# Delta stage: rows normalised and transposed ahead of the systems, and split behind the last substitution step

## What is computed

```python
h = _rms(x, attn_norm_w)
q = silu(silu(_causal_dwconv(h @ Wq.T, conv_q)))   # k and v alike
q = _l2norm(q.reshape(B, T, nh, hd))               # k alike; 32 heads of 16
beta = jax.nn.sigmoid(h @ Wbeta.T)
def step(S, inp):
    kt, qt, vt, bt = inp
    err = jnp.einsum('bhvk,bhk->bhv', S, kt) - vt
    S = S - bt[..., None, None] * err[..., None] * kt[..., None, :]
    o = jnp.einsum('bhvk,bhk->bhv', S, qt)
    return (S, o)
S, o = jax.lax.scan(step, S0, (km, qm, vm, bm))
x = x + _rms(o, out_norm_w) @ Wout.T
```

## Time and profile before

| what | value |
|---|---|
| median of 3 runs | 3093.07 us (3091.05 to 3095.14) |
| profiled execution | 3089.57 us |
| its span | 3087.7 us |
| VectorE busy | 1990.8 us, 64% |
| TensorE busy | 2757.9 us, 89% |
| ScalarE busy | 1436.7 us, 47% |
| GpSimd busy | 1009.8 us, 33% |
| delta phase in the span | from about 570 to 1690 us |

### The profile page before, as it was taken

The page is one execution under the profiler, slowest core; times in us unless marked ns, Lnnn a source line. Parts: engine busy times, 40 slices in busy tenths (PEclk is TensorE's granted clock), DMA queues, the critical chain, the costliest instruction groups (busy, mean ns, idle before and its releaser), DMA issues. The chain is left out here.

```text
span 3087.7 us, 66709 instructions
## 1 busy us (share of the span) xinstructions
PE 2757.9 (89%) x26968; PEld 1466.9 (48%) x26968; DVE 1990.8 (64%) x2991; ACT 1436.7 (47%) x2378; POOL 1009.8 (33%) x713
## 2 busy tenths in 40 slices
PE   6999999686888888888855999999999699999997
PEld 3444444252544444444433444444444366666664
DVE  3444444459989898898993544545543377777775
ACT  2222222375767758667632432222222256666664
POOL 0000000107538346274481000000000177777776
PEclk9999999888998989889866999999999899999998
DMA  6999888500000000000040032332120111111110
GB/s 241 336 334 332 312 284 310 176 15 1 2 29 2 29 13 19 29 2 29 16 155 21 22 111 94 101 104 96 66 71 28 66 38 41 41 41 41 41 37 31
DMA packets 126284, 290.20 MB, mean 94 GB/s; under 512 B 30480, under 2 KB 35216, under 8 KB 121968
## 3 DMA queue, kind: packets, MB, share of 16 engines
q1 hardware_dynamic: 122608, 261.85, 24.4%
q10 hardware_dynamic: 3456, 25.17, 2.4%
HBM read 244.96 MB, written 42.01 MB: 93 GB/s over the span
## 5 line engine op out<-in xcount | busy, mean ns | idle before, releaser
L2141 POOL TENSOR_TENSOR d_zb<-d_za 128x1024 f32<-128x1024 f32 x32 | 75.3, 2354 | 955.7 <-DVE d_za L2203 955.7
L899 PE MATMUL b_e<-b_hT,s_region 128*128 128x512 f16 x1152 | 283.3, 392 | 49.1 <-DVE s_region L1327 36.5
L1629 PE MATMUL c_r<-c_hT,c_g_pair 128*128 128x512 f16 x1056 | 244.4, 382 | 1.6 <-DVE c_hT L1805 1.6
L2008 PE MATMUL d_m<-s_region,d_xiT 128*128 128x512 bf16 x1024 | 238.4, 384 | 5.1 <-ACT d_xiT L2121 1.6
L1629 PE MATMUL c_r<-c_hT,c_u_pair 128*128 128x512 f16 x1056 | 242.3, 379 | 0.0
L1629 PE MATMUL c_d<-c_d_pair,c_aT 128*128 128x512 f16 x1056 | 242.1, 379 | 0.0
L1819 DVE SCALAR_TENSOR_TENSOR c_av<-c_r,c_sg 128x512 f32<-128x512 f32 x88 | 60.8, 691 | 271.7 <-PE c_r L1629 211.2
L1327 DVE SCALAR_TENSOR_TENSOR s_region<-b_e,b_cw,s_region 128x496 f32<-128x496 f32 (+2 forms) x288 | 203.0, 716 | 18.3 <-ACT s_region L1117 9.9
L851 POOL TENSOR_TENSOR b_tmp<-b_L,s_hn 128x496 f32<-128x496 f32 (+30 forms) x124 | 122.5, 988 | 260.9 <-ACT b_L L1100 251.5
L851 POOL TENSOR_TENSOR b_tmp<-b_L,b_U 128x496 f32<-128x496 f32 (+30 forms) x124 | 130.8, 1055 | 223.8 <-ACT b_L L1100 214.4
L899 PEld LDWEIGHTS b_e<-b_hT,s_region 128*128 128x128 f16 x1152 | 104.0, 100 | 190.0 <-DVE s_region L1327 44.2
(11 more groups left out here) (255 smaller groups left out, 6029.7 us busy)
## 6 DMA issues: line engine op xcount, KB each, us to landing
a_cT<-in_ctxT SPq DMA_DIRECT2D x128, 512.0 KB, 9.7
a_cn<-in_ctx SPq DMA_DIRECT2D x128, 512.0 KB, 9.1
a_x_ln<-in_x SPq DMA_DIRECT2D x8, 1024.0 KB, 16.1
a_cw<-in_ctx SPq DMA_DIRECT2D x128, 64.0 KB, 9.5
a_x_res<-in_x SPq DMA_DIRECT2D x32, 256.0 KB, 11.4
x<-a_x_out SPq DMA_DIRECT2D x32, 256.0 KB, 11.3
b_xg<-x SPq DMA_DIRECT2D x8, 1024.0 KB, 5.5
om<-b_hT SPq DMA_DIRECT2D x32, 256.0 KB, 2.0
```

The lines of the kernel that those rows point to most:

```text
L899: mm = pe.matmul(p[:], w_qkv[:, a, i, n, c * P:(c + 1) * P], hp[:, b, n, :], start=(n + a + b == 0), stop=(n == DC - 1 and a == 1))
L1629: mm = pe.matmul(out, x, y, start=start and i == 0, stop=stop and i == 2)
L2008: mm = pe.matmul(p[:], xiT[:, c, :], w[:, c, j * 512:(j + 1) * 512], start=(c == 0), stop=(c == DC - 1))
L2141: nc.gpsimd.tensor_tensor(o[:, :, 0, :], a[:, :, 0, :], a[:, :, 1, :], ALU.add).then_inc(bf, 1)
```

## The change

In the body k of the delta phase:

- PE transposes V0 to V3, then the rows of group k + 1, then waits for the last Gram bank, then L0 to L7. Before, L0 to L4 stood ahead of the rows and L5 to L7 behind.
- ACT copies right sides 0 and 1, normalises the rows of group k + 1, copies right side 2, takes the rows' high halves, copies right side 3 and then systems 0 to 7. Before, all right sides came first, then the normalising, systems 0 to 4, the high halves, eight masks, systems 5 to 7.
- Those eight masks now stand with the next sixteen, behind the first taps and the copies of U.
- VectorE splits the low halves of group k + 2 behind step 30 instead of step 24.

Nothing is added or removed; every instruction has the same shape as before. `LE` is no longer used. The MLP phase is the same in both kernels.

```diff
--- before.py
+++ after.py
@@ -994,13 +994,11 @@
                     pe.wait_ge(vt_ready, DC * (k + 1))
                     for i in range(NV):
                         turned(k, f"V{i}", lambda d: vt[:, :, d])
-                    E.used(pe, 0, f"{k}.gram{DC - 1}.{BG - 1}")
-                    for i in range(LE):
-                        turned(k, f"L{i}", lambda t: Gs[:, t, :])
                 if nxt:
                     rows(g)
                 if cur:
-                    for i in range(LE, NL):
+                    E.used(pe, 0, f"{k}.gram{DC - 1}.{BG - 1}")
+                    for i in range(NL):
                         turned(k, f"L{i}", lambda t: Gs[:, t, :])
                 if nxt:
                     E.used(pe, 0, f"{g}.h{DC - 1}")
@@ -1205,12 +1203,12 @@
                 prev, cur, nxt = k >= 1, 0 <= k < NG, k + 1 < NG
                 g = k + 1
                 if cur:
-                    for i in range(NV):
-                        right_side(k, i)
-                    if nxt:
-                        rows_normal(g)
-                    for i in range(LE):
-                        system(k, i)
+                    right_side(k, 0)
+                    right_side(k, 1)
+                if cur and nxt:
+                    rows_normal(g)
+                if cur:
+                    right_side(k, 2)
                 if nxt:
                     rows(g)
                 if k < 0:
@@ -1219,8 +1217,8 @@
                     high_weights("v")
                     act.wait_ge(w_ready, PAIRED["q"])
                 if cur:
-                    masks(k, 0, 8)
-                    for i in range(LE, NL):
+                    right_side(k, 3)
+                    for i in range(NL):
                         system(k, i)
                 if nxt:
                     tap_first(g, "q", 0)
@@ -1236,7 +1234,7 @@
                 if not cur and prev:
                     squares_first()
                 if cur:
-                    masks(k, 8, 24)
+                    masks(k, 0, 24)
                 if nxt:
                     betas(k)
                     tap_first(g, "q", 1)
@@ -1422,7 +1420,7 @@
                 for s in range(S - 1):
                     if cur:
                         solve(k, s)
-                    if s == 24 and g + 1 < NG:
+                    if s == S - 2 and g + 1 < NG:
                         low_rows(g + 1)
                     if nxt and s == 0:
                         convolve(g, "q", 0)
```

## The result

The changed kernel took 3064.31 us (median of 4 runs, 3061.35 to 3070.18), the kernel before beside it 3094.11 us: a ratio of 0.9907, 95% interval 0.9889 to 0.9924, 29.8 us faster (23.5 to 34.3 by the interval). Forecast were 3066.0 us and 27.1 us. The profiled execution took 3061.35 us, the shortest of the four, and has a span of 3059.6 us, 28.1 less than before.

A forecast was written before the change was run, and what follows sets the result against it. VectorE sets the pace, so only its idle time can be won. Six seams at 3.6 us, first 3.4, last 3.3, less 1.2, give 27.1 us: 3093.07 to 3066.0 us, range 3050 to 3080.

The forecast's parts named there:

- a loss of 1.2: Behind the seam: ScalarE's square and the projection of chunk 3 come late, taken as 0.2 us a cycle in six cycles.
- the late clock: Output projection late in the cycle: at low clock cycles are 3.5 us longer; no more or fewer long cycles expected.
- the allowances: At each seam: 0.5 us for a clock fall and 0.3 for the load's landing, making 4.4 us saved 3.6.
- the ring: Old seam: VectorE's split waits for ScalarE's high halves, and system 7's copy waits for step 29, which stands behind that split.
- ScalarE's chain: At the seam, ScalarE's copies in the new order are next late: 4.4 us saved, not 7.45; VectorE keeps about 3.4 idle.
- The wait for hc: Ahead of normalising the rows: hc lands at 1038.5, deciding by 0.1 us; another seam's load would put 1.4 on the path.
- even odds: TensorE's new 3.4 us pause while rows are normalised: clock falls or not, a fall costing 1.0 us, so 0.5 a seam.
- the slack of system 7's transpose: TensorE at the seam: system 7 turned near 1048.0 against 1048.6 needed, 0.6 us slack, reducing a clock fall's 1.6 us cost.
- Rival B: As the forecast, but the long cycles become short: four more times 3.5 us, 3052 us; chance 0.14.
- C: Win partly given back: clock falls or TensorE's round trip, 1.5 us a seam, or root 1.2 late each cycle; 3078, chance 0.20.
- D: Slower: half clock holds through chunk 0's projections, 10.7 instead of 5.35 us, chunk 3's projection 6.5 late; 3104, chance 0.05.
- E: VectorE starts as ever, system 7's copy held by something the rows do not show; 3087 to 3093, chance 0.05.

The follow-up runs named there:

- the kernel with the later masks: Changed kernel with twelve masks instead of 24 ahead of ScalarE's squares and nineteen instead of seven behind: 3055.0 us, ratio 0.9877; with the eight matmuls 3044.41 us.

## Why the prediction was right

**The sum.** Forecast were 27.1 us, measured 29.8. By VectorE's starts in the profiles the first seam gave 3.35 us (forecast 3.4), the six others with rows 19.8 (21.6 forecast), the last 3.2 (3.3): 26.4 against 28.3. The bodies gave 3.7 us where a loss of 1.2 was forecast, because one long cycle fewer was met. So the mechanism and its sizes held within 2 us, and that the profiled total lies above the forecast and not below it is luck of the late clock.

**The seam.** Its terms came out one by one: right sides 0 and 1 at 0.98 us instead of 0.88, the normalising 2.83 as forecast (2.8), the high halves 2.98 instead of 2.29 (two waits of 0.17 us for TensorE), the eight systems 4.05 instead of 3.90. Start of the next system: forecast 12.8 us behind the first right side at full clock and 13.6 with the allowances, measured 13.60. The 7.45 us wait went and 4.04 us came back at line 1098, where 3 to 4 were forecast. The order with the masks behind gives 26 of the 30 us, the split and the masks by themselves 0 and 5. The prediction named the ring and got ScalarE's chain right; it didn't say that most of its 4.4 us a seam are the 3.4 us of masks.

**The load.** The wait for hc decided as forecast: nothing at four of the six seams, 0.35 and 1.07 us at two, 0.24 on the mean where 0.3 was taken. The seam of 27.3 us is the one with 1.07.

**The clock in the pause.** It fell at all six seams, where even odds were taken, and cost 0.8 where 1.0 was taken. The 0.5 us of the sum was low by 0.3. The cost came by another way than the slack of system 7's transpose: ScalarE waited for the rows' transposes in the high halves.

The prediction read the length of the gap as what decides: 2.52 us in the old seam, followed by full speed "in six seams of seven". The rows don't bear that out. Of the seven it was five, since at the second the 16 transposes took 2.96 us at a granted clock of 0.72. And the other kernels with the old order had the same gap, 2.50 to 2.53 us, at each of the six seams, behind the same instructions: behind it the transposes ran at full speed throughout at all six with the masks alone, at two of six with the split alone, and at none of six with the eight matmuls in the kernel before. So the even odds were a guess and not a reading.

**First and last seam.** 3.3 us at the first and 3.4 in the last cycle (120.2 to 116.8), forecast 3.4 and 3.3; the masks alone bring them. The first one differs between executions of the old order too: 27.3 us in the kernel before, 25.9 and 25.8 with the split alone and with the matmuls.

**Behind the seam.** ScalarE's square was forecast 24.6 us behind the start; TensorE's sums began at 24.5:

```profile
1073.15 1.13 PE L916 MATMUL b_r<-s_xa,b_heads 128*32 128x512 f32 x4 [1.92 <-ACT s_xa L1126]
```

Here a step failed. I took a gap of about 2.6 us ahead of the projection of chunk 3 as one that keeps the clock and set the loss at 0.2 us a cycle. The gap came ahead of the sums instead. It was 1.9 us in five cycles, and behind it the granted clock went to the lower level in four of them (0.58 to 0.61 over the next 4 us). In exactly these four the root came late:

```profile
1100.10 3.35 DVE L1338 RECIPROCAL s_region<-s_region 64x512 f32<-64x512 f32 x1 [0.80 <-ACT s_region L1153]
```

The wait is 0.8 us each. In the two of cycles 2 to 7 in which the clock stayed up there, VectorE did not wait for the root at all. So the odds were wrong. But the wait is not what it costs. Two short cycles have it, the fourth and the fifth, and their bodies are 93.5 us, against 93.2 in the second, which has none, and 93.1 and 93.2 in the short ones before: 0.2 to 0.4 us. The rest comes back in the same body, in part because the wait ahead of the scaling is 0.27 us there instead of 0.46. Where a long cycle has it, as the third and the seventh did, it costs nothing further: the bodies were 96.7 us, as before. In all that is under 1 us, where 1.2 was forecast. The size of the term held by this, and not by its reason. It also fits that the kernel with the later masks, in which the wait is gone, is no faster once the matmuls are in.

**The late clock.** I assumed as many long cycles as in the median run before, and that a cycle once long stays long. In the profiles it was four before and three after, and in the changed kernel two short cycles follow the long third. Eight matmuls that hold the late clock up gave 18 to 20 us in either kernel, of which the profiled cycles show 14.8 and 10.8 (the profiled executions of the two kernels without the matmuls were 3 to 3.5 us below their medians). The late clock is about as heavy in both, so the assumption did little harm, but a win of a few us could be hidden or doubled by it. Rival B was this gain; the change doesn't bring it, eight matmuls bring most of it.

**The rivals.** C's mechanisms were both there: the clock fell at each seam, at 0.8 us and not 1.5, and the root was late in four cycles, at 0.8 us of wait and not 1.2 in each. D's did not occur: the projections of chunk 0 ran at full clock, 5.34 us for 24. E did not occur: nothing that the rows hide held system 7, and its copy came 3.5 us earlier behind the first right side.

The Trainium skill's sentence in "TensorE: Matmul & The Clock Gate", Part 1, that an idle stretch brings the throttled clock back, agrees with this case where TensorE was nearly idle: with the pause nearly empty the clock fell at six seams of six, with four times the transposes in it at three of six. It doesn't tell the seams with the gap of 2.52 us apart.

## What to carry to other kernels

Where two engines wait for each other at a seam, list each engine's order there and ask which copy waits for which step. Taking work off one side gives nothing while the other side's wait grows into its place, and then the win is what left the chain that is next late, not the wait that is seen. Price a seam by that chain, with the pitches of the rows; at the seam worked out it came within 0.1 us. Run the parts in pairs too and not only alone: here split and masks each looked like next to nothing, and their pair is the one that was not run. And look for cycles of two lengths before timing such a change: a passage that finds the clock now up and now down moves the whole by more than the edit.

## What the runs showed of the hardware

A gap of 1.9 us on TensorE among outer products of 32x32 was followed by the lower clock in four cycles of five. A gap of 2.50 to 2.53 us in the old seam, behind the same instructions each time, was followed by full speed at five seams of six in the kernel before, six of six with the masks alone, two of six with the split alone and none of six with the eight matmuls. So the length of a gap didn't tell which it would be, nor did the instructions just ahead of it.

Eight matmuls in a pause of 1.8 to 2.9 us, run at the lower clock for part or all of their time, were worth 18.4 us of 3093 in the kernel before, with no other edit. The passage that counts then ran at full speed in six cycles of six there, and in four of six in the changed kernel.
